# Last cross attention: a turn's values product and totals in one run at its head

## The reference, cut to what matters

```python
q = split_heads(x @ Wq) * 64 ** -0.5            # 16 heads of 64
k, v = split_heads(context @ Wkv)
k = concatenate((null_kv[0], k)); v = concatenate((null_kv[1], v))   # 1602 keys
attn = softmax(q @ k.T)
out = (attn @ v) @ Wout
return layer_norm(out, 1e-6) * ln_scale + ln_bias
```

## Time and profile before

| | |
|---|---|
| median of 3 runs | 4162.15 us (4161.4 to 4168.01) |
| the profiled execution: its time, its span | 4164.39 us, 4162.6 us |
| TensorE busy | 3682.6 us, 88% |
| VectorE, ScalarE, GpSimd busy | 2920.0, 2281.2, 1622.6 us |
| mean granted clock of TensorE | 0.937 |
| first to last peak transposes of the changed stretch | 2094.72 to 3871.43 us |

### The profile page before, as it was taken

How to read it: one execution, slowest core, us unless ns; L and a number is a source line. 1 busy time by engine, 2 the same in 40 slices (tenths; PEclk the granted TensorE clock), 3 DMA queues, 4 the chain that set the end, 5 groups by cost and what they waited for, 6 DMA issues and landing times. The chain is left out here.

```text
span 4162.6 us, 72200 instructions
## 1 busy us (share of the span) xinstructions
PE 3682.6 (88%) x28017; PEld 2207.6 (53%) x28017; DVE 2920.0 (70%) x4526; ACT 2281.2 (55%) x3856; POOL 1622.6 (39%) x1655
## 2 busy tenths in 40 slices
PE   3699999889699976997799999999999999999654
PEld 2233333478344434674466666666666666666441
DVE  5799999544577736553377777777777777777747
ACT  2599999633377751222166665665655665655320
POOL 3011111320011104220067667677767667667310
PEclk7699999999799987998899999999999999999877
DMA  4432232002155301000100000000000000000010
GB/s 139 128 60 52 51 59 45 17 18 55 47 86 90 50 2 31 2 2 10 63 1 17 1 17 1 14 4 1 17 1 17 1 17 1 1 1 1 7 36 20
DMA packets 117717, 122.89 MB, mean 30 GB/s; under 512 B 19008, under 2 KB 95648, under 8 KB 116992
## 3 DMA queue, kind: packets, MB, share of 16 engines
q1 hardware_dynamic: 104184, 111.20, 12.1%
q10 hardware_dynamic: 13200, 7.16, 0.6%
HBM read 102.51 MB, written 15.68 MB: 28 GB/s over the span
## 5 line engine op out<-in xcount | busy, mean ns | idle before, releaser
L869 DVE TENSOR_REDUCE att_peak.1<-psS 128x1 f32<-128x512 f32 (+1 forms) x1024 | 579.1, 633 | 19.8 <-PE psS L744 13.5
L2188 POOL TENSOR_TENSOR key_sums_0.1<-key_sums_0.1,prob_0.1 128x512 f32<-128x512 f32 x256 | 439.7, 1717 | 28.7 <-POOL key_sums_0.1 L2188 0.4
L2188 POOL TENSOR_TENSOR key_sums_1.1<-key_sums_1.1,prob_1.1 128x512 f32<-128x512 f32 x256 | 421.3, 1646 | 28.7 <-ACT prob_1.1 L2038 0.4
L839 ACT ACTIVATE att_probT.1<-psT 128x512 f32<-128x512 f32 (+1 forms) x682 | 366.6, 568 | 29.1 <-PE psT L773 9.8
L2097 DVE TENSOR_TENSOR att_highest.1<-att_highest.1,prob_0.1 128x1024 f32<-128x1024 f32 (+1 forms) x160 | 274.0, 1712 | 128.5 <-ACT prob_0.1 L2032 121.5
L2097 DVE TENSOR_TENSOR att_highest.1<-att_highest.1,prob_1.1 128x1024 f32<-128x1024 f32 (+1 forms) x160 | 278.1, 1738 | 114.3 <-ACT prob_1.1 L2032 107.5
L869 DVE TENSOR_REDUCE att_peak.2<-psS 128x1 f32<-128x512 f32 (+1 forms) x512 | 261.7, 568 | 78.7 <-PE psS L744 75.8
L790 PE MATMUL psM<-att_probT.1,quad_values.1 128*9 128x256 f32 (+1 forms) x3840 | 291.9, 382 | 0.2 <-issue 0.2
L2118 DVE TENSOR_TENSOR prob_0.1<-prob_0.1,psO 128x1024 f32<-128x1024 f32 (+1 forms) x256 | 244.0, 1016 | 49.0 <-PE psO L1948 49.0
L2118 DVE TENSOR_TENSOR prob_1.1<-prob_1.1,psO 128x1024 f32<-128x1024 f32 (+1 forms) x256 | 243.9, 1016 | 49.0 <-PE psO L1948 49.0
L744 PE MATMUL psS<-key_stack.1,query_stack.1 64*128 64x512 bf16 (+1 forms) x1024 | 253.5, 379 | 27.2 <-PEq L379 18.2
(11 more groups left out here) (689 smaller groups left out, 7826.3 us busy)
## 6 DMA issues: line engine op xcount, KB each, us to landing
key_stack.1<-key_parts SPq DMA_DIRECT2D x384, 58.0 KB
key_stack.2<-key_parts SPq DMA_DIRECT2D x96, 200.1 KB
ctx_rows.1<-in_ctx_dram SPq DMA_DIRECT2D x8, 1536.0 KB
key_parts<-split_parts.2 SPq DMA_DIRECT2D x8, 1200.8 KB, 7.6
ctx_keys_0.1<-in_ctx_dram ACTq DMA_DIRECT2D x4, 768.0 KB
ctx_keys_1.1<-in_ctx_dram ACTq DMA_DIRECT2D x4, 768.0 KB
query_stack.1<-query_parts SPq DMA_DIRECT2D x192, 16.0 KB
ctx_values_0.1<-in_ctx_dram SPq DMA_DIRECT2D x4, 768.0 KB
```

The lines of the kernel that those rows point to most:

```text
L839: self.k.nc.scalar.activation(probs[:, blks[0]:blks[-1] + 1, :].rearrange("p b q -> p (b q)"), bank[0:w, 0:len(blks) * S], ACT.Exp).then_i ...
L869: self.k.nc.vector.tensor_reduce(self.peak[:, 2 * h + s, c:c + 1], self.score_bank[m % 3][:, 0:w], AX_X, ALU.max).then_inc(self.peak_done. ...
L2188: nc.gpsimd.tensor_tensor(acc, acc, own[:, h, c * BANK:(c + 1) * BANK], ALU.add).then_inc(self.summed.sem, 1)
```

## The change: what it does, and the diff

- TensorE does all 7 meets of turn i-2 at the head of iteration i, the totals right behind them, then the peaks of turn i-1; groups 0 to 3 have only projections and scores (and the spread).
- The totals go to the right half of psT[1], the bank of the values product, and no longer to psO; two waits that guarded psO go (in `pe_turn_peak` and in `pe_total`).
- ScalarE takes the eight exponentials of a turn two in each group; before, four in group 0 and four in group 1.
- VectorE takes the reciprocal right after `dve_shift`, the divide after the second lowering of head 1, and its raises 2 and 3 stand before the last two lowerings and around the taking at place 3.

Nothing is added to or left out of the arithmetic.

```diff
--- before.py
+++ after.py
@@ -1775,7 +1775,6 @@
     CHUNKS = (KB + 1) // 2
     NULL = KTAIL + 1
     KEYS = KB * P
-    MEETS = [range(0, 2), range(2, 4), range(4, 6), range(6, 7)]
 
     def __init__(self, k, mem):
         self.k = k
@@ -1931,8 +1930,6 @@
     def pe_turn_peak(self, pe, i):
         nc = self.k.nc
         pe.wait_ge(*self.peaked(i + 1))
-        if i >= 2:
-            pe.wait_ge(*self.inverted(i - 1))
         if i >= 1:
             pe.wait_ge(*self.lowered(8 * i))
         for h in range(2):
@@ -1949,12 +1946,10 @@
         last.then_inc(self.spread.sem, 1)
 
     def pe_total(self, pe, i):
-        nc = self.k.nc
+        k, nc = self.k, self.k.nc
         pe.wait_ge(*self.summed(14 * (i + 1)))
-        if i + 1 < self.TURNS:
-            pe.wait_ge(*self.lowered(8 * (i + 2)))
         for h in range(2):
-            last = nc.tensor.matmul(self.peaks[h * self.HD:(h + 1) * self.HD, 0:S], self.ones[:], self.acc[i % 2][:, h, 0:S],
+            last = nc.tensor.matmul(k.psT[h * self.HD:(h + 1) * self.HD, 1, S:2 * S], self.ones[:], self.acc[i % 2][:, h, 0:S],
                                     start=True, stop=True)
         last.then_inc(self.totalled.sem, 1)
 
@@ -1980,14 +1975,13 @@
             self.pe_project(pe, ("ctx", 0, n))
         for i in range(-1, T + 3):
             scores, softmax, meets = 0 <= i < T, 0 <= i - 1 < T, 0 <= i - 2 < T
+            if meets:
+                for s in range(self.CHUNKS):
+                    self.pe_meet(pe, i - 2, s)
+                self.pe_total(pe, i - 2)
+            if softmax:
+                self.pe_turn_peak(pe, i - 1)
             for g in range(4):
-                if meets and g == 2:
-                    self.pe_total(pe, i - 2)
-                if meets:
-                    for s in self.MEETS[g]:
-                        self.pe_meet(pe, i - 2, s)
-                if softmax and g == 0:
-                    self.pe_turn_peak(pe, i - 1)
                 for name in self.due(i, 2 * g):
                     self.pe_project(pe, name)
                 if softmax and g == 0:
@@ -2054,9 +2048,9 @@
                     for s in self.of_run(g):
                         self.act_keep(act, i, s)
                 self.act_take_at(act, i, 2 * g + 1)
-                if softmax and g < 2:
-                    for part in range(4):
-                        self.act_exp(act, i - 1, g, part)
+                if softmax:
+                    for part in (2 * g, 2 * g + 1):
+                        self.act_exp(act, i - 1, part // 4, part % 4)
 
 
 
@@ -2121,7 +2115,7 @@
         dve.wait_ge(*self.totalled(i + 1))
         if i >= 1:
             dve.wait_ge(*self.out_done(i))
-        self.k.nc.vector.reciprocal(self.rtotal[:], self.peaks[:, 0:S]).then_inc(self.inverted.sem, 1)
+        self.k.nc.vector.reciprocal(self.rtotal[:], self.k.psT[:, 1, S:2 * S]).then_inc(self.inverted.sem, 1)
 
     def dve_divide(self, dve, i):
         b, p = divmod(i, self.PAIRS)
@@ -2140,6 +2134,8 @@
             scores, softmax, meets = 0 <= i < T, 0 <= i - 1 < T, 0 <= i - 2 < T
             if softmax:
                 self.dve_shift(dve, i - 1)
+            if meets:
+                self.dve_invert(dve, i - 2)
             self.dve_take_at(dve, i, 0)
             if softmax:
                 for part in range(4):
@@ -2149,23 +2145,22 @@
             if softmax:
                 self.dve_lower(dve, i - 1, 1, 0)
                 self.dve_lower(dve, i - 1, 1, 1)
+            if meets:
+                self.dve_divide(dve, i - 2)
             self.dve_take_at(dve, i, 2)
+            if scores:
+                self.dve_raise(dve, i, 2)
+            self.dve_take_at(dve, i, 3)
+            if scores:
+                self.dve_raise(dve, i, 3)
             if softmax:
                 self.dve_lower(dve, i - 1, 1, 2)
                 self.dve_lower(dve, i - 1, 1, 3)
-            if scores:
-                self.dve_raise(dve, i, 2)
-                self.dve_raise(dve, i, 3)
-            self.dve_take_at(dve, i, 3)
             self.dve_take_at(dve, i, 4)
-            if meets:
-                self.dve_invert(dve, i - 2)
             if scores:
                 self.dve_raise(dve, i, 4)
                 self.dve_raise(dve, i, 5)
             self.dve_take_at(dve, i, 6)
-            if meets:
-                self.dve_divide(dve, i - 2)
             if scores:
                 self.dve_raise(dve, i, 6)
                 self.dve_peak(dve, i)
```

## The result

4365.02 us, median of 4 runs (4362.99 to 4373.07), against 4164.4 for the kernel before beside it: ratio 1.048, interval 1.0465 to 1.0496. The change costs 4.8%. It was forecast as slower, at 4448 with a range from 4310 to 4510. The direction and the mechanism are as forecast, the likeliest value is 83 us too high.

A forecast was written before the change was run, and what follows sets the result against it. TensorE, busy 88%, was taken as the bound, with GpSimd's sums holding it after the change. 4162 us plus 176 for waits plus 110 for the clock gave 4448, range 4310 to 4510 for 8 in 10.

The forecast's parts named there:

- TensorE's gain: Values product in one run, fewer changes of array shape: TensorE's own work in a plain turn falls from 27.49 to 26.2 us.
- The price of a change of shape: On TensorE, 0.19 us per change of array shape; six of 16 a turn go, taken as 1.0 us.
- The rival that rested on it: TensorE stays the bound and GpSimd's sums keep up: 26.2 us a turn, about 4085 us; chance 0.06.
- The wait for the sums: Totals ahead of the peaks wait for GpSimd's key sums: plain turn 29.8 us; all waits together +176 us.
- The clock: TensorE's holes before the totals lower its granted clock: 2.0 us a plain turn, 1.4 the others, about +110 us.
- Divide: In 7 output turns VectorE's divide waits, delaying the product's copy and TensorE's next value projection: 35.2 against 30.81, +4.4 us.
- The exps: Head 1's first exp comes later than GpSimd is ready: 0.2 to 0.5 us in plain turns; about +2.8 in context turns.
- the forecast case itself: Both the wait for the sums and the fallen clock: 4448 us, own range 4385 to 4515; chance 0.60.
- rival 2: The wait comes as worked out but the clock does not fall, or only in few turns: 4338 us; chance 0.22.

The follow-up runs named there:

- experiment 3: Changed kernel with GpSimd's additions of chunks 4 and 5 cut from 512 to 8 columns, shortening the key sums: 4125.23 us, ratio 0.9901 to the kernel before.
- 8: Kernel of experiment 1 with the totals moved to group 1, between value projection and scores: 4118.6 us, ratio 0.9887 to the kernel before.
- experiment 1: Changed kernel with totals, reciprocal and divide put back in the middle of the turn: 4112.31 us, 4106.63 in a second session; ratios 0.9878 and 0.9856.
- experiment 2: Changed kernel with 12 more matmuls that nobody reads, between the meets and the wait for the sums: 4312.3 us, ratio 1.0358 to the kernel before.
- experiment 5: Changed kernel with the divide moved back behind the output product's copy, in front of the fourth maximum: 4353.02 us, ratio 1.0449 to the kernel before.
- experiment 4: Changed kernel with exponentials four and four again, head 0 in group 0, head 1 in group 1: 4287.68 us, ratio 1.0297 to the kernel before.

## Why the prediction was right, and where its sizes were off

- *TensorE's gain.* Worked out 26.2 us for a plain turn of its own; 26.37 stood there once nothing held it (experiment 3). The price of a change of shape, 0.19 us, came back in 8, but not as one price for all: the twelve changes of a turn in experiment 1, eleven in 8 and ten in 3 go with 26.59, 26.40 and 26.37 us. The Trainium skill (TensorEngine Tiling (Array Packing), Key Properties) states that changing the tiling mode drains the engine. The trace agrees in that turns with fewer changes are shorter. The rival that rested on it, 4085 us, is near what comes (4103 to 4112) when the totals are put elsewhere.
- *The wait for the sums.* Shown by 1 and by 3, which take it away in different ways. 29.8 us forecast for a plain turn at full clock, 29.30 measured: the sums took 21.2 instead of 21.7, the total and its change 0.64 instead of 0.65. The term of 176 us was 128: 69 in the plain turns with the first and last against 86, 26 in the output turns against 31, and 33 in the 21 context turns against 59, the part that was most mis-sized. At full clock the three kinds of context turns take 30.85, 30.48 and 29.58 us, not 31.3 to 31.7. There head 1's exp let GpSimd wait 1.1 to 2.8 us, near the forecast, but head 1's sums took 9.06 us behind it, where the forecast leaves some 10, because most maxima had by then been done beside head 0.
- *The clock.* The term was forecast as 110 us and measured as 76, what 128 leaves of the 204.4 us of the stretch, and what experiment 2 gives. 59 are late starts of GpSimd, 9 the spells in the middle of five output turns, for which the prediction had no term, and some 8 totals and peaks that ran at half speed. The size failed, and each factor of it was too large: the hole was 2.83 us in a plain turn, not 3.5, and 2.0 in the others, not 2.5 to 3.1; the clock was down for one spell of 3.41 us at most places, not for up to 5.1; the price of a spell behind the stop was 1.6 us, not 2.0; and only 9 of the 28 shorter stops had one. I had taken the length of the spell from the two longer holes of the earlier trace rows, 3.7 and 3.8 us, when the 2.7 us hole in the same rows was nearer.
- *Divide.* 4.4 us forecast for the output turns, 3.7 without loss of clock. 1.65 of them are the divide (5). The rest is the wait for head 1's exp and the sums behind it: in experiment 5 GpSimd still rests from P+19.9 to P+24.8 between the heads of the output turn shown. That this rest is the exps' was not tried alone.
- *The exps.* "0.2 to 0.5 us, partly in the 29.8 already" in plain turns: nothing was found, head 0's sums end at P+19.6 there and the exp is done by P+18.7.
- *The range.* That it held owes something to luck. Both terms of the sum were too large, by 48 and 34 us, and the range of the forecast case itself, 4385 to 4515, was missed (its ends, added up from its own bounds, would be 4382 and 4520; that is missed too). The measured time is inside 4310 to 4510 because the lower end was drawn down for rival 2, the wait without loss of clock. That rival is out as well: the clock fell, and its wait was 128 us and not 176.

## What to carry to other kernels

An instruction of an in-order engine inherits the wait of whatever stands in front of it: before one is moved forward, read when its last input is ready, here P+28.8 against a turn of 27.5, and how much slack it had at the old place. An engine at 39% can set the pace of one at 88% when a loop of dependences runs through it (here the sums of a turn wait for its exps, these stand behind its peaks, and the peaks behind the totals, which wait for the sums of the turn before): add start, length and hand-over of the slow helper and compare with the period, not its busy share. And idle time of TensorE has a second price, above all if it comes in one piece: filling the hole with useless matmuls made the kernel faster by some 50 us.

## What the runs showed of the hardware

- In the changed kernel's stretch the granted clock was down for 171 us in all. Of the 28 stops of 2.0 us before totals 9 had a spell of low clock beside them, of the 32 of 2.8 us all had. A spell behind the stop cost GpSimd's start 1.6 us (9.07 against 7.44 us after the peaks).
- Idle time in pieces of at most 1 us (experiment 4) left the clock up in about two of three plain turns, at the same length of turn (29.26 us against 29.30); in the others it fell too, within a few us of the three pieces of 0.99, 0.26 and 0.70 us, so small holes close together count as well. The Trainium skill (TensorE: Matmul & The Clock Gate, "What's actually happening") has the gate follow how busy the array lately was. Both the stops and the small holes agree with that.
- In the changed kernel GpSimd's seven additions of a head took 12.2 us beside five maxima (head 0) and 9.05 us beside the last one and the fold to 256 columns (head 1), 8.45 alone; both heads together took 21.2 there and 21.4 before, however the maxima were distributed. VectorE's maxima with both inputs in SBUF and GpSimd's additions hold each other up: a maximum took 1.22 us where no addition ran beside it, and 2.11 between additions in the turn from 2783.06; an addition took 1.27 us in that turn with no maximum beside it, and up to 2.22 with one. Why they do was not tried.
